# A graph layer's messages: one maximum over 2560 columns, or five over 512 between the other steps of a group

## The reference

```python
z = (z - mean) * jax.lax.rsqrt(var + BN_EPS) * gamma + beta
msg = jax.nn.sigmoid(z[:, :H]) * jax.nn.softplus(z[:, H:])
agg = jnp.zeros_like(node_feats).at[src].add(msg)
return node_feats + agg
```

## Time and profile before

| | |
|---|---|
| median of 3 runs | 3820.1 us (3819.95 to 3830.05) |
| profiled execution, its own time | 3820.0 us |
| its span, first to last instruction | 3818.3 us |
| busy in the span: PE, DVE, ACT, POOL | 3044.3, 2763.0, 2218.7, 2573.1 us |
| chunk stage, 2288 to 2926 us: DVE, ACT, PE busy | 580.9, 589.5, 445.9 us of 638 |

### The profile page before, as it was taken

How to read it: one execution, slowest core, us unless ns; L and a number is a source line. 1 busy time by engine, 2 the same in 40 slices (tenths; PEclk the granted TensorE clock), 3 DMA queues, 4 the chain that set the end, 5 groups by cost and what they waited for, 6 DMA issues and landing times. The chain is left out here.

```text
span 3818.3 us, 83823 instructions
## 1 busy us (share of the span) xinstructions
PE 3044.3 (80%) x18854; PEld 2156.6 (56%) x18855; DVE 2763.0 (72%) x7466; ACT 2218.7 (58%) x6111; POOL 2573.1 (67%) x2634
## 2 busy tenths in 40 slices
PE   6875999999988999999999976767776577767661
PEld 2322333333336777777777765656665466666661
DVE  6567888888875555555555548999998688888787
ACT  1423999999984666666666659989996010000003
POOL 2667777777776777777777760028887677777770
PEclk8986999999999999999999997888987789888885
DMA  7433333333336888888888884557774433333321
GB/s 201 129 109 100 108 101 108 102 106 107 101 95 200 264 263 264 264 263 263 263 263 264 260 296 172 200 196 275 275 270 133 112 81 77 80 80 80 75 69 41
DMA packets 315282, 640.18 MB, mean 168 GB/s; under 512 B 54446, under 2 KB 188759, under 8 KB 306999
## 3 DMA queue, kind: packets, MB, share of 16 engines
q0 software_dynamic: 99584, 247.90, 22.8%
q1 hardware_dynamic: 173416, 267.88, 22.4%
q10 hardware_dynamic: 42192, 123.38, 8.8%
HBM read 425.59 MB, written 213.37 MB: 167 GB/s over the span
## 5 line engine op out<-in xcount | busy, mean ns | idle before, releaser
L372 POOL DMA_INDIRECT rec_d<-arena x830 | 798.9, 963 | 345.0 <-issue 335.0
L871 POOL DMA_INDIRECT arena<-b_tab,arena x880 | 832.3, 946 | 281.1 <-issue 262.3
L783 PE MATMUL psum<-arena 128*128 128x440 f16 x3360 | 720.5, 352 | 50.5 <-ACT arena L466 50.0
L892 DVE TENSOR_TENSOR arena<-psum,arena 128x512 f32<-128x512 f32 x440 | 283.5, 686 | 544.1 <-DMA arena<-b_tab,arena 303.5
L634 DVE TENSOR_SCALAR arena<-iota_t,arena 128x880 f16<-128x880 f16 x840 | 523.8, 666 | 109.6 <-PE psum L783 102.6
L982 PE MATMUL psum<-weT,arena 128*128 128x256 f32 x1760 | 545.1, 392 | 45.3 <-DVE arena L892 41.9
L466 ACT ACTIVATE arena<-arena 128x128 f16<-128x128 f16 x1680 | 561.7, 386 | 0.0
L783 PEld LDWEIGHTS psum<-arena 128*128 128x128 f16 x3360 | 288.2, 97 | 477.1 <-issue 160.6
L1596 PE MATMUL psum<-arena,x_sb 128*128 128x129 f32 x2368 | 329.4, 304 | 158.8 <-DVE x_sb L1483 105.7
L1475 DVE TENSOR_TENSOR arena<-psum,arena 128x258 f32 x880 | 374.7, 426 | 83.6 <-PE psum L1596 77.5
L985 PE MATMUL psum<-arena 128*128 x2640 | 432.5, 273 | 0.0
(11 more groups left out here) (265 smaller groups left out, 5574.7 us busy)
## 6 DMA issues: line engine op xcount, KB each, us to landing
z_d<-arena ACTq DMA_DIRECT2D x220, 512.0 KB
arena<-z_d SPq DMA_DIRECT2D x44, 2560.0 KB
arena<-rec_d SPq DMA_DIRECT2D x220, 260.0 KB
arena<-in_edge_attr SPq DMA_DIRECT2D x83, 640.0 KB, 4.8
arena<-early_d SPq DMA_DIRECT2D x36, 516.0 KB
arena<-b_tab,arena POOLq DMA_INDIRECT x880
rec_d<-arena POOLq DMA_INDIRECT x831, 2.1
early_d<-arena POOLq DMA_DIRECT2D x9, 1032.0 KB, 5.2
```

Of the source, the lines that this page charges most:

```text
L372: nc.gpsimd.indirect_dma_start(rec_rows, bass.IndirectOffsetOnAxis(e_idx[:, s, k:k + 1], 0), e_buf[:, s, k, :], None).then_inc(s_es[s], 16)
L783: last = nc.tensor.matmul(bank(4 + 2 * k + h)[:, 0:HALF], hot_lane[:, s, k, :], hot_tile[:, s, h * HALF:(h + 1) * HALF], start=start, stop ...
L871: nc.gpsimd.indirect_dma_start(bg[:, s, k, :], None, b_tab, bass.IndirectOffsetOnAxis(rec[:, s, k, H:H + 1].bitcast(I32), 0)).then_inc(s_b ...
```

## The change

VectorE's maximum is cut into five operations, one per group. Each is followed by the group's addition, a wait for the operation's own result, the product and the one-hots, so the addition also changes places with the product. `s_spl` now counts 220 operations instead of 44, and ScalarE's wait ahead of L1319 counts five per chunk: it is for all five operations of the chunk two before.

```diff
-                        wait(act, s_spl, c + (i - 1))
+                        wait(act, s_spl, CG * c + (CG * i - CG))
                         nc.scalar.activation(ex[:, i, :, :], v, ACT.Sigmoid, bias=stat[:, 5:6], scale=stat[:, 4:5]).then_inc(s_q, 1)
...
                     dve.wait_ge(s_lg, c + 1)
                     dve.wait_ge(s_v, c + 1)
-                    nc.vector.scalar_tensor_tensor(v, ex[:, j % 2, :, :], -1.0, v, ALU.mult, ALU.max).then_inc(s_spl, 1)
                     dve.wait_ge(s_sig, c + 1)
                     before = not (isinstance(c, int) and c == 0)
                     if before:
                         firsts = adds(c - 1)
-                    dve.wait_ge(s_spl, c + 1)
                     for g in range(CG):
-                        nc.vector.tensor_tensor(u[:, g, :], u[:, g, :], v[:, g, :], ALU.mult).then_inc(s_msgT, 1)
+                        nc.vector.scalar_tensor_tensor(v[:, g, :], ex[:, j % 2, g, :], -1.0, v[:, g, :], ALU.mult, ALU.max).then_inc(s_spl, 1)
                         if before:
                             add(c - 1, (j - 1) % CS, g, firsts[g])
+                        dve.wait_ge(s_spl, CG * c + (g + 1))
+                        nc.vector.tensor_tensor(u[:, g, :], u[:, g, :], v[:, g, :], ALU.mult).then_inc(s_msgT, 1)
                         hots(c, g)
```

## The result

The changed kernel takes 4115.8 us (median of 5 runs, 4114.2 to 4118.3) against 3820.1: 1.0769 times as long, 95% interval 1.0754 to 1.0783. The forecast was 4124, range 4085 to 4160. The profiled execution spans 4114.1 us, 295.8 more than before.

A forecast was written before the change was run, and what follows sets the result against it. The chunk stage was taken as bound by a ring between VectorE and ScalarE, growing from 27.23 to 42.76 us a pair; +292.2, +13.1 and +4.8, less 6 for GpSimd, on 3820.0 gave 4124 us, range 4085 to 4160.

The forecast's parts named there:

- The ring: Chunk stage: VectorE and ScalarE wait on each other in turn; one turn per pair of chunks, 27.23 us before, 42.76 after.
- the fifth part: Last of a chunk's five maximum operations on VectorE; ends 10.56 us after the chunk's first addition, then ScalarE's L1319 may start.
- The pause: Pause of 12.5 us for the early normalisation in the chunk stage; the pair distance containing it becomes 46.0 us.
- The sum: Chunk stage: pair distances +292.2, first distance +13.1, last pair +4.8, together +310; less 6 for GpSimd gives 4124 us.
- GpSimd was to give back 6: GpSimd's early gathering, which ended after x1's rows were stored, is done in time in a longer chunk stage: -6 us.
- parts of 0.69: Upper bound for one of the maximum's five operations on VectorE, against 0.60 us taken: +14 us on the time.
- parts of 0.56: Lower bound for one of the maximum's five operations on VectorE, against 0.60 us taken: -6 us on the time.
- only ScalarE's second wait counts: Rival: additions find their products ready, so a pair takes 35.4 us and the kernel 3971 us; chance 0.09.
- the waits stay covered: Rival: fifth parts are done before ScalarE reaches L1319, so the kernel is not slower, 3813 us; chance 0.03.
- The lower clock: TensorE at 1.2 GHz after idling; 2.4 GHz in the second link would take 0.9 us less per pair, -18 in all.
- the second link: Second chunk of a pair: from ScalarE's copies through TensorE's transpose and product to VectorE's addition, 4.05 us.
- moves the end by as much: Whatever the chunk stage loses shifts the kernel's end equally, since GpSimd's gathers pace the stage after it.

The follow-up runs named there:

- e5: Changed kernel, with ScalarE's copies of a pair's first chunk ahead of the first waiting sigmoid of v instead of behind it: 4062.3 us.
- e6: Changed kernel, with TensorE filling the gap ahead of each chunk's fifth transpose with extra unused clears to keep its clock at 2.4 GHz: 4074.7 us.
- e7: Changed kernel, with VectorE loading the five block numbers of the additions ahead of its waits for the logarithm: 4112.4 us in a single run.
- e1: Kernel before, with the maximum cut into five operations of 512 columns, all together at the chunk's head, product and addition in old order: 3809.9 us, ratio 0.9978.
- e8: Kernel before, with ScalarE's scaling of v of a pair's first chunk moved ahead of the second sigmoid of v: 3816.0 us, ratio 1.0000.
- e9: Kernel before, with the edits of e1 and e8 together: 3809.9 us, ratio 0.9952 to the kernel before, 3830.3 on that chip.
- e10: Kernel before, with the maximum as two operations (1024 and 1536 columns) together at the chunk's head: 3822.4 us in a single run, against 3830.3.
- e2: Changed kernel, with the product ahead of the addition again in each group: 4106.6 us, ratio 1.0754 to the kernel before.

## Why the prediction was right

*The ring* was right in its shape and in nearly each term. A pair takes 42.64 us in the quoted one, 42.4 in the mean, against 42.76. From the first addition to the end of the fifth part it is 10.45 against 10.56: a part adds 0.60, as taken, but product, addition and one-hots take 1.99 instead of 2.02. From copies to addition 4.17 and 4.09 against 4.10 and 4.05; ScalarE's waits 5.9 and 9.6 against some 6 and 10. The pause behaved as said: VectorE's first parts around it stand 44.5 us apart (2600.31 to 2644.78) plus the 1.4 by which the first of them is late behind its loads, 45.9 against 46.0.

*The sum* was 8 us high. The chunk stage was to grow by 310; from the first maximum to the store of x1 it grew by 302 (2304.1 to 2946.2 before, 2306.7 to 3251.0 after). GpSimd was to give back 6; it gave 10, some 5 because its own end is no longer behind the store and nearly 5 of the store, which takes 21.9 us from its start to SyncE's next load (3251.0 to 3272.9) instead of 26.6. The 8 that I had put into the range for the store and taken as nothing was half there. These two make 12; against them stand 2.6 us by which the stage starts later and 0.9 behind the first late gather. Two bounds of the range were reckoned a little wide: by the formula for the fifth part, parts of 0.69 give some 12 and not 14, parts of 0.56 some 5 and not 6.

*The rivals.* That only ScalarE's second wait counts (3971) fell with e5: the first counts 53 us by itself. That the waits stay covered fell with the 318 us of L1319. The lower clock was taken at its full price in the second link, and e6 shows that this was right: at 2.4 GHz the two links fall by 1.3 us each, more than the 0.9 that the prediction had for one.

*What was wrong in the text* without harm to the number: VectorE idles 2.0 us ahead of the first chunk's addition, not 3.3, because its first part comes 1.4 us late behind the loads of block numbers; e7 shows that this lies under TensorE's link. And the price of five parts was seen on VectorE alone: e1 says that they help GpSimd by 37 us. The changed kernel gets more of that, an early gathering of 361 us (2657.0 to 3018.0) instead of 423, and cannot use it, since its GpSimd then waits 252 us for the store.

*Where the expectations failed*: e1 (+8 expected, -10 measured) and e8 (-8 expected, 0 measured) fail on the sentence that whatever the chunk stage loses "moves the end by as much", read for a shorter stage too. That holds for a longer stage. For a shorter one it doesn't: GpSimd's early gathering had its end 6 us behind the store, which was in my sum as a gain of 6 and should have been read as a second bound. In e1 the ring also grew by 0.2 us a pair and not by 0.4, and the store of x1 was not late at all. The expected times of e9 and e10 were missed upward; e2 to e7 came out in their ranges.

What stays open: why the eleven runs of e8 spread over 13 us, and why in e1 and e10 some gathers stood through all parts while most got through.

## What to carry to other kernels

When an operation is cut and spread, ask who waits for its last part: another engine that needs the whole is released only when the last part is done, and everything queued behind that wait moves with it. A busy share that doesn't change while the stage grows by half says that the loss is in such a ring; add up one turn of it, from row to row, and the sum is the period. And where two chains end a stage within a few microseconds, look at both before pricing an edit: here the edit to the earlier one (e8) did not move the next stage's start, the edit to the later one (e1) moved it by 12 us, and both together by 21.

## What the runs showed of the hardware

A gather on GpSimd that meets one long VectorE operation with two SBUF inputs stands still until it is over: up to 3.5 us beside the 2.8 us maximum, 9.6 to 10.0 us beside the 6.7 us addition L1511 and what follows it, instead of 0.94. Between five short operations most get through (73 of 77 in e1 stay below 1.5 us): 423, 406 and 386 us of early gathering with one, two and five operations of the same work behind each other, 361 with the five spread out. Five operations of 512 columns lasted 3.10 us together against 2.82 for one of 2560.
